# A gather stage in which POOL stops waiting for PE's sums and ACT's index copy waits for them instead

## The reference

```python
xw = x @ W                       # W: 256 x 64
norm = dinv[s] * dinv[d]
out = jax.ops.segment_sum(norm[:, None] * xw[s], d, num_segments=n)
return out + b
```

## Time and profile before

| | |
|---|---|
| median of 3 runs | 8538.8 us |
| span of the profiled execution, its own time | 8571.6 us, 32.8 us over that median |
| POOL busy, all stages | 3872.1 us (45% of the span) |
| PE busy, all stages | 5243.7 us (61%) |
| first and last gather of this stage | 4247.5 and 6804.2 us |
| gathers of this stage | 1664, 1677.9 us busy, 886.8 us idle before them |
| copies of sums of this stage (L2332) | 208, 78.8 us busy |

### The profile page before, as it was taken

How to read it: one execution, slowest core, us unless ns; L and a number is a source line. 1 busy time by engine, 2 the same in 40 slices (tenths; PEclk the granted TensorE clock), 3 DMA queues, 4 the chain that set the end, 5 groups by cost and what they waited for, 6 DMA issues and landing times. The chain is left out here.

```text
span 8571.6 us, 116878 instructions
## 1 busy us (share of the span) xinstructions
PE 5243.7 (61%) x30143; PEld 3895.7 (45%) x30144; DVE 4536.6 (53%) x8737; ACT 3218.8 (38%) x7600; POOL 3872.1 (45%) x3841
## 2 busy tenths in 40 slices
PE   2999577777776677456623334332222247699999
PEld 2554455555555555346512212121111136588888
DVE  5555677777777777543423333343333389843333
ACT  0554566666666666311200000010000057543333
POOL 1221566666666666342366666676666413200000
PEclk7999899999999999788756666655555579789999
DMA  5554777777777777551322222222222468710000
GB/s 141 208 211 175 228 211 212 210 212 210 212 210 212 212 211 210 142 162 48 115 55 64 64 61 66 61 83 73 78 73 74 83 196 282 233 42 14 13 12 12
DMA packets 539832, 1154.93 MB, mean 135 GB/s; under 512 B 121739, under 2 KB 273458, under 8 KB 532798
## 3 DMA queue, kind: packets, MB, share of 16 engines
q0 software_dynamic: 217216, 691.51, 28.1%
q1 hardware_dynamic: 299864, 438.79, 16.0%
q10 hardware_dynamic: 22480, 21.44, 0.8%
HBM read 878.85 MB, written 280.36 MB: 135 GB/s over the span
## 5 line engine op out<-in xcount | busy, mean ns | idle before, releaser
L2231 POOL DMA_INDIRECT g_row<-y_parts,g_index x1664 | 1677.9, 1008 | 886.8 <-issue 666.8
L965 POOL DMA_INDIRECT ae_kv<-edge_table,ae_index x1664 | 1607.4, 966 | 1042.2 <-PE psum L1183 451.3
L1183 PE MATMUL psum<-ae_kv,ae_edge_hot 128*128 128x266 f32 x3328 | 882.4, 410 | 451.1 <-ACT ae_step_sums L1073 279.7
L1152 PE MATMUL psum<-ae_q,ae_node_hot 128*128 x3328 | 923.4, 440 | 75.0 <-DMA ae_q<-queries 50.4
L1183 PEld LDWEIGHTS psum<-ae_kv,ae_edge_hot 128*128 128x128 f32 x3328 | 617.7, 195 | 690.4 <-ACT ae_step_sums L1073 365.0
L2254 PE MATMUL psum<-g_row,g_keep 128*128 128x64 bf16 x4992 | 312.2, 218 | 862.3 <-issue 688.6
L1152 PEld LDWEIGHTS psum<-ae_q,ae_node_hot 128*128 128x128 f32 x3328 | 720.1, 221 | 217.2 <-issue 95.0
L1007 DVE TENSOR_TENSOR ae_kv<-ae_kv,psum 128x2048 f32<-128x2048 f32 x208 | 475.9, 2288 | 630.8 <-remote 591.3
L2427 DVE TENSOR_TENSOR g_acc<-g_acc,g_step_sums 128x64 f32 x832 | 188.0, 226 | 919.6 <-issue 699.7
L2254 PEld LDWEIGHTS psum<-g_row,g_keep 128*128 128x128 bf16 x4992 | 247.2, 114 | 926.3 <-issue 781.0
L3144 ACT ACTIVATE em_h<-psum,experts_affine 128x256 f32<-128x256 f32 (+1 forms) x800 | 404.9, 556 | 610.5 <-PE psum L3101 431.5
(11 more groups left out here) (595 smaller groups left out, 10358.9 us busy)
## 6 DMA issues: line engine op xcount, KB each, us to landing
ae_node_hot<-rel_rows SPq DMA_DIRECT2D x208, 512.0 KB
edge_hots<-g_keep SPq DMA_DIRECT2D x208, 356.0 KB
gn_hots<-edge_hots SPq DMA_DIRECT2D x208, 356.0 KB
gn_row<-source_places SPq DMA_DIRECT2D x208, 256.0 KB
ae_kv<-edge_table,ae_index POOLq DMA_INDIRECT x1664
g_row<-y_parts,g_index POOLq DMA_INDIRECT x1664
pair_sums<-gn_out SPq DMA_DIRECT2D x624, 4.0 KB
x_sorted<-nt_x SPq DMA_DIRECT2D x52, 128.0 KB
```

Source lines behind the costliest of these rows:

```text
L965: g.indirect_dma_start(out=kv[:, s, n, :], out_offset=None, in_=dram["table"], in_offset=bass.IndirectOffsetOnAxis(ap=index[:, s, n:n + 1] ...
L1152: ins = t.matmul(bank[n // 2][:, (n % 2) * D:(n % 2 + 1) * D], oht[:, s, n * P:(n + 1) * P], qb[:, bass.ds(at[n // 2], 1), :].rearrange("p ...
L1183: ins = t.matmul(bank[4 + m % 2][:, 0:CW], ohs[:, n, :], kv[:, s, n, KC:2 * D], start=n % 2 == 0, stop=n % 2 == 1)
L2231: g.indirect_dma_start(out=row[:, m, n, :], out_offset=None, in_=table, in_offset=bass.IndirectOffsetOnAxis(ap=index[:, m, n:n + 1].bitcas ...
```

## The change

Three lines in all. POOL no longer waits for `made[m]`, only for the index columns. ACT waits for `made[m]` of group k before it copies the index columns of group k + 8, where it waited for it after them. So POOL can still not overwrite rows whose sums aren't made: the index columns that let it go are copied only once they are.

```diff
             def gather(i, m):
                 g.wait_ge(index_ready, i * S + m + 1)
-                wait_count(g, made[m], i)
                 wait_alone(g, gate)
                 for n in range(G):
...
             def copy(i, s):
                 for ii, m in groups_of(i, s):
+                    a.wait_ge(made[m], ii + 1)
                     if not isinstance(ii, int) or ii + 1 < GROUPS // S:
                         a.wait_ge(gathered[m], ii * 16 * G + 16 * G)
                         a.wait_ge(hot_made[m], ii + 1)
                         columns_of((ii + 1) * S + m, m)
-                    a.wait_ge(made[m], ii + 1)
```

## The result

Twenty runs of either kernel: before 8556.96 us in the median (8517.15 to 8624.79), after 8601.12 us (8566.83 to 8623.85). The ratio is 1.0038 with a 95% interval of 1.0020 to 1.0056, so the change costs 33 us (17 to 48); the two medians stand 44 us apart, which lies inside that interval. The profiled execution after has a span of 8598.4 us and a time of 8600.32 us, at a granted clock of 0.805.

The account below looks back on a forecast made before the run. POOL's chain of gathers was taken to bound the stage; 56 gaps by 0.45 us added 25.2 us, all other terms 0, to 8538.8 us: 8564 us (8596.8 us profiled), range 8528 to 8592 us.

Parts of the forecast that it names:

- POOL's chain bounds the stage: Gather stage: POOL's 1664 gathers, busy 1677.9 us and idle 886.8 us before them, fill the stage.
- its wait alone gives nothing: Dropping POOL's wait for the sums gains nothing: ACT awaits the same signal at 56 gaps; at 19 it had come.
- The link: At 56 gaps that start with PE's signal, ACT's index copy now precedes the gather: 0.45 us each, 25.2 us (21 to 36).
- Late gaps 0: At 19 gaps where ACT comes after the sums are made, index copy and gather stand where they stood: 0.
- groups without a gap 0: At 125 groups without a gap the nearest margins are 1.1 us and more, so 0.45 us makes no new gap: 0.
- the prediction's own signs: Expected: gaps 1.02 us after index copy's start, first half near 50 summing to about 190 us, second half about 3 us different.
- ACT's other work covered: ACT's work behind the signal comes 0.3 us later, covered by POOL's 20 us of gathers; uncovered, 17 us at 56 places.
- The measure: Runs lie 32.8 us below the profiled span at their median, so 8538.8 + 25.2 = 8564 us.
- The rule weighed: POOL's later start against DVE's burst shortens stretched gathers by 0.1 us a gap: 8558 instead of 8564 us.
- Absorbed: Rival: PE uses POOL's added idleness to finish sums, so the next gap shrinks; 8539 to 8550 us, chance 0.25.
- Faster: Rival: POOL's later start lets PE finish sums before slowing, 12 gaps of 3.3 us vanish; 8524 us, chance 0.14.
- ACT in the way: Rival: ACT is busy at most of the 56 signals, each costing about 1.0 us; 8595 us, chance 0.11.

Follow-up runs that it names:

- all three pairs of kernels: Order before against changed order: unforced (8556.96, 8601.12 us), POOL held one group ahead of the sums (8422.99, 8476.33 us), PE's sums made late (8613.48, 8662.98 us).
- late sums: PE begins a pair's sums only once gathers seven groups further on have landed: on the kernel before 8613.48 us, on the changed kernel 8662.98 us.
- one group ahead: POOL held to one group ahead of PE's sums instead of eight: 8422.99 us with the order of the kernel before, 8476.33 us with the changed order.
- old order: ACT's and POOL's order of waits as in the kernel before; with PE's sums made late 8613.48 us, ratio 1.0039.

## Why the prediction was right, step by step

**POOL's chain bounds the stage; its wait alone gives nothing.** The first half is right: the stage took 25.9 of the span's 26.8 us. The second half stays argued: the kernel in which POOL waits for both met no gaps, and shows only that the second wait costs nothing there.

**The link.** The mechanism was right and the size too large. I took 0.45 us, above the 0.37 that 1.02 less 0.65 gave, for the two further waits that ACT passes. They cost nothing: the index copy starts 0.13 us after the signal, the copy of sums did so after 0.12. The link is 0.35 us at the usual gap in all three pairs of kernels (0.77 to 1.12 us), just under the 0.37 us that I had called the lower bound, because POOL starts 0.99 us after the index copy and not 1.02. (The forecast's range began at 0.3 us a gap, below its own lower bound.) With 52 gaps where I had 56 it is 18 us, not 25.2.

**Late gaps 0, groups without a gap 0.** The late gaps are as long as they were (10.1 us in the mean in both traces), but there are 20 and not 19, and this one gap is 10 us. The signal gaps grew by 16.9 us in sum, which looks like 52 links of 0.35 us and is not: four gaps fewer take away some 13 us, and the 52 are longer by 0.58 us in the mean, of which the link is 0.34. The remaining 0.24 us a gap (13 us in all) stays unexplained; one gap of 9.29 us, at 5436.7, is a good part of it. With one more late gap (11 us), 1 us more in the gathers and some 3 us less between gathers of a group this gives the stage's 25.9 us, which look like my 25.2. So the hit on the sum is luck in good part: the link accounts for 18 us of it.

By the prediction's own signs the mechanism stands and the steadiness of the gaps doesn't. All 72 gaps end 0.99 or 1.00 us after the start of their index copy, and the first half has 46 gaps, over the 45 that would have spoken for another theory. But the first half's sum is 181.5 us and not 190, the second half gained 9.7 us and not 3, and 29 of the 72 gaps stand at groups that had none, which was named as a sign of being wrong. Whether the change moves gaps about, or two executions of one kernel differ as much (single runs spread over 108 us), can't be told from one trace of each. The late gaps did not occur in any kernel of the experiments, so they stay untested.

**ACT's other work covered.** Right as far as it could be seen: three idle copies behind the copy of sums cost nothing, ratio 1.0001, but POOL had no gaps in these runs. With gaps, in the late sums, the mean gap grew by 0.38 us and the mean link by 0.37, which leaves next to nothing for it.

**The measure.** The forecast took 8538.8 us from three runs as its base and put the 32.8 us between it and the profiled span down to profiling. A profiled execution is its span and 2 us (8598.4 and 8600.32); the 32.8 us were spread between runs. So the 8601 us lie above the 8564 us and above the range's upper end, though the difference (33 us, 17 to 48) holds the forecast's 25.2, and the ratio on the forecast's own base gives 8571 us. The step that failed is the base (8538.8 us, 18 us below the median of twenty), not the change.

**The rule weighed.** The gathers did not get shorter: 1677.9 us became 1678.9. Where many gaps move alike the effect is there with either sign, 15.2 us shorter one group ahead and 7.8 us longer with late sums. The Trainium skill (SBUF — State Buffer, "SBUF: two separate sides") says that of DVE and GpSimd the one that starts first holds the shared port pair for its whole instruction, and the other waits. The gathers agree with that (1.59 us when started inside the one-hots, 0.99 us when under way before them), though no view shows who held the ports. What I made of it, a gain in proportion to the later start, was wrong, because what counts is which gather starts inside the one-hots.

**The rivals.** Absorbed: this gave at most 11 us over the base, and the interval starts at 17. With prompt sums 0.90 us more of link gave 0.90 us more of gap. That PE gives nothing back where it steps slowly was not tested by itself; there are four signal gaps fewer. Faster: refuted, 52 signal gaps remained of 56, with a larger sum. ACT in the way: refuted, since POOL starts 1.12 us after the signal at the usual gap and 0.99 us after the index copy started, ACT took the signal up within 0.13 us. That its 8595 us lie nearer to 8601 than the forecast's 8564 comes from the base.

**What the prediction lacked.** A rival in which POOL has no gaps at all. That decided more than any other: with gaps 1.0038, without them 0.9997.

## What to carry to other kernels

An operation put between a signal and the engine that bounds a stage costs its link (here 0.35 us, the small copy's start to the next engine's start less what the direct wait took) times the number of times that this engine runs dry. Where a group of gathers or more covered it, it cost nothing that could be seen here (ratios 0.9997 and 0.9999). So count the gaps first, and read the link between events and not from durations. If the gaps come from something that varies between executions, the traces of two kernels have their gaps at different places and their sums agree or differ by chance. Then measure the change once more with the gaps forced, as here by holding the producer one group ahead: 53 us over runs that spread by 4 to 10 us tell more than 33 us over runs that spread by 100.

## What was not expected of the hardware

The same program ran in two ways 12% apart: 8517 to 8626 us in 37 runs of the kernel before, 7633 to 7649 us in 69. Every set of runs taken together was of one kind, and one chip gave both in different sets. The expectations that speak of a kind of chip were wrong in that. The difference in the traces is PE's pace while POOL issues gathers. In the kind with gaps PE's small matmuls come singly or in twos with 0.5 to 1.2 us of idle before them (5057.21 to 5060.07 above), and for 56 groups of the kernel before its signal comes only when POOL is dry; in the kind without, 24 of them take 0.86 us beside POOL's gathers. POOL's idle in this stage is 911.6 against 513.6 us, and before the attention stage's gathers (L965) 1045.3 against 547.2. When PE is made to do its sums with POOL dry (late sums, old order) the runs spread by 14 us and not 100, at nearly the same time. The granted clock doesn't tell the kinds apart in this stage: it is 0.62 and 0.53 in the halves of the changed kernel with gaps (above), and 0.63 and 0.53 without:

```profile
3695.00:4790.00 1095.00, 438.69 (x3228) 287.98 (x3228) 431.17 (x1165) 111.04 (x421) 837.87 (x845) 0.63 0.29 75
4790.00:5890.00 1100.00, 315.30 (x2848) 224.61 (x2846) 468.52 (x1363) 116.27 (x495) 845.65 (x820) 0.53 0.36 89
```

What sets the kind, and why PE slows, stays open: no edit here switched it.
